# Clipped parts and mask of a gated output computed with a second operand, a spread column

## The reference

```
x = x + relu(adj @ (item @ W_item.T + b_item) + layernorm(x) @ W_user.T + b_user)
h = layernorm(x)                                    # 10000 x 128, padded capacity C per expert
probs = softmax(h @ gate_w + gate_b); idx = argmax(probs); prb = probs[idx]
hmid = relu(buf[e] @ w1[e] + b1[e]); ybuf[e] = hmid @ w2[e] + b2[e]      # rows sorted by expert
y = ybuf[idx, pos] * (prb * kept)
y = nan_to_num(y, nan=0.0, posinf=1e4, neginf=-1e4)
x = x + y
```

## Time and profile before

| | us |
|---|---|
| median of 3 runs | 1349.24 (1348.21 to 1349.49) |
| the profiled execution's own time | 1349.4 |
| its span on the core | 1347.6 |
| PE busy | 1315.5 (98%) |
| DVE busy | 1186.8 (88%) |
| ACT busy | 946.0 (70%) |
| POOL busy | 541.0 (40%) |

### The profile page before, as it was taken

One profiled execution on the slowest core, in us unless ns is written; L12 is line 12 of the kernel. 1 busy time (PEld: TensorE's weight loads), 2 busy tenths in 40 slices (PEclk: granted clock), 3 DMA queues, 4 the chain that ended last, 5 costly groups with the idle time before them and its releaser, 6 DMA issues.

```text
span 1347.6 us, 19720 instructions
## 1 busy us (share of the span) xinstructions
PE 1315.5 (98%) x6050; PEld 1083.7 (80%) x6050; DVE 1186.8 (88%) x1824; ACT 946.0 (70%) x927; POOL 541.0 (40%) x335
## 2 busy tenths in 40 slices
PE   7999999999999999999999999999999999899994
PEld 6888888888888888888888888888888887677773
DVE  7999989898898998989989899898898988677875
ACT  5777767767677676776767768767677675777772
POOL 0001053250431514415235052350532636778887
PEclk9999999999999999999999999999999999999997
DMA  8999999999999999999999999999999996333210
GB/s 329 353 380 405 412 397 396 379 376 385 369 376 379 378 381 377 372 375 373 387 365 381 373 377 373 382 370 385 364 383 376 373 367 239 109 96 100 68 49 4
DMA packets 97007, 441.84 MB, mean 328 GB/s; under 512 B 26685, under 2 KB 34919, under 8 KB 96961
## 3 DMA queue, kind: packets, MB, share of 16 engines
q1 hardware_dynamic: 69017, 418.17, 81.5%
q0 software_dynamic: 21984, 12.87, 3.8%
q10 hardware_dynamic: 5960, 10.24, 2.3%
HBM read 428.11 MB, written 24.16 MB: 336 GB/s over the span
## 4 chain that ended last, share of the span: by engine, by line
PE 94%; issue 2%; DVE 1%; POOL 1%; DMA 1%; ACT 0%; SPq 0%; POOLq 0%; DVEq 0%; ACTq 0%
PE bank L1146 26%; PE bank L1148 26%; PE bank L1157 26%; PE bank L1267 5%; PE bank L1255 2%; PE bank L1256 2%; PE bank L1257 2%; PE bank L1129 1%; PE bank L1192 1%; POOL out L1114 1%; PE bank L1241 1%; PE bank L1278 1%; PE bank L1174 1%; DMA raw<-records 1%; PE bank L1182 0%
## 5 line engine op out<-in xcount | busy, mean ns | idle before, releaser
L711 DVE TENSOR_TENSOR a_lo<-raw,a_hi 128x2000 fp32r<-128x2000 f32 (+1 forms) x400 | 864.0, 2187 | 76.6 <-ACT a_hi L516 74.5
L516 ACT CAST a_hi<-raw 128x2000 fp32r<-128x2000 f32 (+1 forms) x400 | 723.7, 1826 | 274.5 <-PE bank L1148 172.1
L1146 PE MATMUL bank<-a_hi,h_hi 128*128 128x500 f32 x1560 | 613.9, 394 | 0.2
L1148 PE MATMUL bank<-a_hi,h_lo 128*128 128x500 f32 x1560 | 606.2, 389 | 0.0
L1157 PE MATMUL bank<-a_lo,h_hi 128*128 128x500 f32 x1560 | 418.3, 389 | 0.0
L1146 PEld LDWEIGHTS bank<-a_hi,h_hi 128*128 128x128 f32 x1560 | 293.9, 188 | 58.6 <-issue 1.2
L1157 PEld LDWEIGHTS bank<-a_lo,h_hi 128*128 128x128 f32 x1560 | 293.4, 188 | 59.0
L1148 PEld LDWEIGHTS bank<-a_hi,h_lo 128*128 128x128 f32 x1560 | 294.4, 189 | 56.4
L1039 POOL TENSOR_TENSOR late<-ve,neghalf 125x4 f32<-125x4 f32 x20 | 55.3, 2763 | 617.9 <-DVE ve L728 617.8
L1114 POOL DMA_INDIRECT out<-raw x104 | 143.4, 1379 | 37.7 <-issue 32.5
L1053 POOL DMA_INDIRECT out<-late,kept_out x76 | 134.9, 1775 | 23.1 <-issue 23.1
(11 more groups left out here) (135 smaller groups left out, 842.9 us busy)
## 6 DMA issues: line engine op xcount, KB each, us to landing
raw<-adj_m SPq DMA_DIRECT2D x380, 1000.0 KB, 6.6
raw<-adj_m SPq DMA_DIRECT2D x20, 500.0 KB
xT<-x_t ACTq DMA_DIRECT2D x20, 250.0 KB
late<-items_t SPq DMA_DIRECT2D x19, 256.0 KB, 4.6
raw<-records SPq DMA_DIRECT2D x24, 191.8 KB
xb<-x ACTq DMA_DIRECT2D x20, 224.0 KB
raw<-w SPq DMA_DIRECT2D x8, 258.5 KB
raw<-w SPq DMA_DIRECT2D x8, 256.0 KB
```

The costliest lines, as they stand in the source:

```text
L516: last = nc.scalar.copy(a_hi[:, g % HI_RING, 0:m], raw[:, g % RAW, 0:m])
L711: last = v.tensor_tensor(a_lo[:, g % RAW, 0:m], raw[:, g % RAW, 0:m], a_hi[:, g % HI_RING, 0:m].bitcast(F32), ALU.subtract)
L1146: nc.tensor.matmul(acc[q][:, 0:BLOCK], h_hi[:, k * HID:(k + 1) * HID], a, start=(k == 0), stop=False)
L1148: last = nc.tensor.matmul(acc[q][:, 0:BLOCK], h_lo[:, k * HID:(k + 1) * HID], a, start=False, stop=False)
```

## The change

Four cells of the tile `xst`, free after the last layer norm of the inputs, become constants: 0, 1e4, -1e4 in the first three, and a row of zeros beside them. The clipped parts and the mask take their second number from one of these columns, spread over the width of the unit, instead of from the instruction. The row numbers are copied by adding the zeros, after the addition of the row and not ahead of it, and the semaphore `yout_ready` is raised by the copy. The constants are written by DVE in the last block, between groups 5 and 6.

```diff
+            def set_limits():
+                for c, value in enumerate((0.0, CLIP, -CLIP)):
+                    v.memset(xst[:, 0, c:c + 1], value).then_inc(limits_set, 1)
+                v.memset(xst[:, 1, :], 0.0).then_inc(limits_set, 1)
...
                     if is_last(b):
                         if g == 4:
                             add_x(b - 1)
+                        if g == 5:
+                            set_limits()
...
+            def limit(c, d):
+                return xst[0:SLOT_P, 0, c:c + 1].broadcast_to([SLOT_P, d])
...
-                v.tensor_scalar(pos, yf, 0.0, CLIP, ALU.max, ALU.min)
-                v.tensor_scalar(neg, yf, 0.0, -CLIP, ALU.min, ALU.max)
-                v.tensor_scalar(mask, yf, 0.0, 0.0, ALU.mult, ALU.not_equal).then_inc(y_parts, 1)
+                if not fixed or n == 0:
+                    dve.wait_ge(limits_set, 4)
+                v.scalar_tensor_tensor(out=pos, in0=yf, scalar=0.0, in1=limit(1, d), op0=ALU.max, op1=ALU.min)
+                v.scalar_tensor_tensor(out=neg, in0=yf, scalar=0.0, in1=limit(2, d), op0=ALU.min, op1=ALU.max)
+                v.scalar_tensor_tensor(out=mask, in0=yf, scalar=0.0, in1=limit(0, d), op0=ALU.mult,
+                                       op1=ALU.not_equal).then_inc(y_parts, 1)
...
-                v.tensor_scalar(tokq[:, u, 0:t].unsqueeze(2).bitcast(U32), recq[:, r, 0:t, C_TOK:C_TOK + 1].bitcast(U32),
-                                0, None, ALU.add)
                 v.tensor_tensor(yout[:, u, 0:t, :], yf.rearrange("p (j d) -> p j d", j=t), recq[:, r, 0:t, 0:HID],
-                                ALU.add).then_inc(yout_ready, 1)
+                                ALU.add)
+                v.tensor_tensor(tokq[:, u, 0:t].unsqueeze(2).bitcast(U32), recq[:, r, 0:t, C_TOK:C_TOK + 1].bitcast(U32),
+                                xst[0:SLOT_P, 1, 0:t].unsqueeze(2).bitcast(U32), ALU.add).then_inc(yout_ready, 1)
```

More of the change, by code:

```diff
@@ L294, in build @@
         y_parts = sem("y_parts")
+        limits_set = sem("limits_set")
         order_ready = sem("order_ready")
```

## The result

The changed kernel takes 1351.83 us (median of 15 runs, 1349.58 to 1354.30) against 1349.28 of the kernel before beside it (15 runs, 1346.75 to 1350.84): a ratio of 1.0019 with a 95% interval of 1.0011 to 1.0026, that is +2.5 us (+1.5 to +3.5). The forecast had +1.2. The time lies within its range, and the change was to be under 0.2%, which it is by its middle. But it is slower beyond its interval, and by about twice as much as the sum said. The two profiled executions lie 4.2 us apart (spans 1347.6 and 1351.8), which is too much for the change. Of this 1.9 us had arisen before DVE's `place` for block 19 (1155.45 before, 1157.37 after), ahead of any changed operation but the four memsets.

A forecast was written before the change was run, and what follows sets the result against it. PE was taken to bound the steady part, DVE the join, and POOL's 13 transfers after unit 28 the end. +0.79 + 0.77 - 0.35 = +1.2 us gave a median near 1350.4 us, range 1348.8 to 1352.6.

The forecast's parts named there:

- POOL still collides: Rival, 6%: one DVE hit of 0.55 us on units 0 and 28, POOL's 0.35 not saved; 1351.9 us.
- Unit 0 through PE, +0.79: Where the layers meet: three longer DVE operations in unit 0 start PE's `turn_slots` of unit 4 0.79 us later.
- the join is hidden: Rival, 14%: ACT's rows for unit 4 come later and cover unit 0's +0.79 wholly or partly; 1349.7 us.
- Unit 28 on DVE, +0.77: At the end: unit 28's clipped part lasts 0.77 us longer on DVE, delaying POOL's last 13 transfers.
- The price of the operations: On DVE: each new operation takes 0.56 us at 384 columns and 0.69 at 512, like an addition.
- The rival of half the rate: Rival, 4%: new operations run at half throughput and DVE becomes the bound; 1367 us.
- Waits for POOL: New operations not held by POOL, nothing gained there; POOL's last 13 transfers no longer stretched, -0.35 us at the end.
- The copy: Row numbers copied after the addition: semaphore goes up 0.76 us after the pair's start, as before; zero.
- the wait for the limits: Met long before; in the loop one more queue instruction under DVE's idle time, none in unit 28; zero.
- the memsets: Four small memsets on DVE in the last block, about 0.3 us; zero effect, at most +0.3.
- It does nothing: Rival, 4%: the new operation runs as fast as the old and is held as often; 1349.2 us.
- the rival of PE's clock: Rival, 4%: PE's longer pause at the join doubles the stretch at 1.2 GHz, +1.1 us; 1351.5 us.

The follow-up runs named there:

- experiment 3: The changed kernel with the old tensor_scalar operations back in unit 0 alone; ratio 1.0015 to the kernel before, +2.0 us.
- experiment 4: The changed kernel with the old tensor_scalar operations back in units 28 to 31 alone; ratio 1.0014 to the kernel before.
- experiment 2: The changed kernel with the three limits in a PSUM bank, so the new operations have one SBUF operand; ratio 1.0018 to the kernel before, about +2.4 us.
- experiment 1: The changed kernel with the three old tensor_scalar operations back everywhere, the rest of the change left in; ratio 0.9999 to the kernel before.
- experiment 5: The changed kernel with the old copy of the row numbers, ahead of the addition; ratio 1.0029 to the kernel before, +3.9 us, 6 runs.
- Experiment 7: The kernel before with unit 0 cut in two on DVE, `split_w1` and `slots_low` right after its gate product; ratio 0.9996 to the kernel before.
- experiment 6: The changed kernel with unit 0 cut in two on DVE, `split_w1` and `slots_low` right after its gate product; ratio 1.0015 to the kernel before, +2.0 us.

## Why the prediction was right or wrong

**The forecast as a whole.** The change was slower, as forecast, and inside the range. That it was inside is in part luck: the sum's own terms end at 1350.4, and the upper end was set by a hold on DVE and a longer stretch at the low clock, of which neither occurred. The rival "POOL still collides" gave 1351.9, next to the measured 1351.83, by terms that did not occur either.

**Unit 0 through PE, +0.79.** Right: +0.78 in the changed kernel, gone again in experiment 3. It did not hang on the 0.01 us between DVE and ACT's rows: in the other six profiles with DVE's unchanged order ACT's rows were ready 0.4 to 2.8 us ahead of DVE. So "the join is hidden" did not happen.

**Unit 28 on DVE, +0.77.** Right as a duration (+0.79), wrong as a term that stands alone. It was counted as if POOL went on waiting for unit 28; experiment 4 shows that in the changed kernel it does not.

**The price of the operations.** Right: 0.56 and 0.69 us, by the columns of the small ones. The rival of half the rate does not occur. The sentence of the Trainium skill (Vector Engine (DVE) Microarchitecture Reference, section 7) does not hold for this form: with two float32 sources, one of them spread, 512 columns take 694 ns, as long as an addition.

**"Waits for POOL", -0.35.** This is the step that failed: in its place the last 13 transfers took 0.20 us more and the first of them started 0.59 us later behind unit 28. It had two parts. That the new operations are never held is right. From "All 32 additions of L990 lie between 558 and 694 ns, that is, none was ever held" I concluded that two operands in SBUF and POOL do not meet. The row answers who holds DVE; it says nothing of who holds POOL, and POOL's own rows were read with the wrong partner: the transfer of 1.58 us at 1327.55, which I wrote to the account of the old form, began inside L998, the addition of two SBUF operands:

```profile
1327.39 0.55 DVE L998 TENSOR_TENSOR raw<-raw 124x384 f32<-124x384 f32 x1
```

1327.94 - 1327.68 = 0.26, and 1.58 - 1.32 = 0.26. The one of 1.41 us at 1334.32 began inside the predicated copy. Of the 27 long transfers before, 19 began in L990, L992 or L998, which the change leaves in, and 8 in L986 or L987; so the old form does stretch transfers, but not those two. The term was not -0.35 but +0.20, and because each of the three operations now holds POOL too, its transfers before unit 28 took all its time and it came 0.59 us late. In brackets I had written that the longer transfers before unit 28 only make POOL wait longer: true of before, and false as soon as 3.8 us more of them use up POOL's slack, some 0.3 to 0.4 us in each expert.

Counted on POOL alone the account is shorter. The first transfer of unit 4, before and after:

```profile
1190.16 1.32 POOL L1114 DMA_INDIRECT out<-raw  x1 [2.69 <-issue]
```

```profile
1193.17 1.62 POOL L1129 DMA_INDIRECT out<-raw  x1 [2.34 <-issue]
```

From there to the end of the last transfer it is 155.30 us before and 156.52 after, +1.22: the holds grew by 3.25 us, and some 2.0 us of that went into waits for DVE that POOL had before and no longer has. The other +1.09 lies between the gate of unit 0 and that transfer (32.55 and 33.64 us); 0.78 of it is unit 0's, and what makes the last 0.3 was not tested.

The rule of the Trainium skill that I set against the row (SBUF — State Buffer, Who interferes with whom: an operation with two SBUF inputs contends with a GpSimd instruction that reads SBUF) holds here: the trace agrees with 45 transfers held for 10.0 us, and experiment 2 takes the second SBUF input of three operations away and with it their effect. As a rival, "POOL still collides" had the right resource and the wrong victim: it priced DVE being held.

**The rest.** The copy, the wait for the limits, the memsets and the record loads were put at zero, and the profiles of experiments 1 and 5 show nothing that speaks against it. "It does nothing" did not happen. Nor did the rival of PE's clock: the stretch at the lower level behind the join is 3.41 us long before and after (1163.21 to 1166.62, and 1165.55 to 1168.96). Its price was read too low, since the window of the earlier trace rows starts 1.09 us behind its start: at half the clock 3.41 us cost some 1.7 us of PE's work (an estimate), not 1.1. The sum in its own terms should have been 0.79 + 0.79 + 0.59 + 0.20 = +2.4.

## What to carry to other kernels

Where two engines meet at a resource, read both sides: for each of the two, compare its short and its long instructions and ask what the other was doing when each began. An engine that is not the bottleneck but has only some tenths of a microsecond of slack in a period can be turned into one by waits that each look like noise; add up its idle time for a period before a cost is written off to it. And a row that shows "never held" is no evidence of "never holds".

## What the runs showed of the hardware beyond that

How a DVE operation holds a transfer of POOL could be read to 0.1 us. One with two operands in SBUF that began before the transfer holds it to its own end; one that begins after it does not, and DVE is not slowed by either in the changed kernel. The profile of experiment 1 has one exception among its 103 transfers, where the operation began only 0.05 us ahead:

```profile
1185.83 0.77 DVE L1004 TENSOR_TENSOR raw<-raw 124x512 f32<-124x512 f32 x1
1185.88 1.32 POOL L1128 DMA_INDIRECT out<-raw  x1 [0.30 <-issue]
```

The transfer is not held, and the operation takes 0.77 us where its like take 0.69. With the old form of one SBUF operand both directions occur. The eight transfers above were held by it, and it is held itself: the mask of 0.90 us in the earlier trace rows ended when POOL's transfer had ended, and experiment 1 has it in unit 0 as well, beside a scatter of POOL.

PE's granted clock behind the pause at the join did not follow the length of the pause. Six of the nine profiles have a stretch of 3.41 us at 0.50 there, the level of 1.2 GHz, as this one of the kernel before (length, PE, PEld, DVE, ACT, POOL, clock, DMA share, GB/s):

```profile
1163.21:1166.62 3.41, 3.41 (x14) 3.41 (x13) 3.26 (x10) 3.41 (x10) 2.80 (x3) 0.50 0.13 30
```

Experiment 7 has 6.83 us at this level, from 1155.44 on, ahead of the place of the pause. Experiments 1 and 6 have none there. Experiment 1, then the changed kernel:

```profile
1164.30:1186.80 22.50, 22.50 (x107) 16.97 (x107) 15.83 (x38) 17.45 (x39) 17.80 (x14) 1.00 0.42 118
```

```profile
1164.30:1186.80 22.50, 21.16 (x95) 16.70 (x96) 15.36 (x36) 14.79 (x33) 16.44 (x13) 0.92 0.35 96
```

Experiment 1 paused for 2.51 us, longer than the kernel before with its 2.23, and kept 1.00, the level of 2.4 GHz. It went from the join to unit 28 in 154.86 us, the others with DVE's unchanged order in 156.1 to 156.5. The 1.5 us between them are near the 1.7 that the missing stretch would give; but no experiment set the clock, and why it was kept stays open. The difference is as large as two of the terms argued over here, so profiles with and without such a stretch should not be compared by their ends.
